# The last 64 channels of the shared expert: high and low rows stacked in one 128-row tile

## The reference

```python
x = x + tanh(g_xattn) * attention(layernorm(x), ctx, ctx, mask)      # 32 heads of 16, 8 groups, causal
x = x + tanh(g_ffn)   * moe(layernorm(x))

# moe, for the 2048 tokens xt (T x 512)
scores  = softmax(xt @ Wg.T)                                         # 16 experts, 4 groups, top 2 groups, top 4
y = sum over the 4 chosen experts e of weight_e * (silu(xt @ W1_e.T) * (xt @ W3_e.T)) @ W2_e.T   # 352 channels
z = (silu(xt @ Ws1.T) * (xt @ Ws3.T)) @ Ws2.T                        # shared expert, 704 channels
moe = y + z
```

## Time and profile before

| | us |
|---|---|
| median of 3 runs | 1259.67 (1258.76 to 1261.95) |
| profiled execution | 1258.79 |
| its span, first to last instruction | 1257.0 |
| PE busy in the span | 1219.0 (97%) |
| PE weight loads busy | 916.7 (73%) |
| VectorE (DVE) busy | 637.5 (51%) |
| ACT busy | 574.3 (46%) |
| POOL busy | 625.3 (50%) |
| `stage_shared` on PE | about 460 to 686 |

### The profile page before, as it was taken

The page is one execution under the profiler, slowest core; times in us unless marked ns, Lnnn a source line. Parts: engine busy times, 40 slices in busy tenths (PEclk is TensorE's granted clock), DMA queues, the critical chain, the costliest instruction groups (busy, mean ns, idle before and its releaser), DMA issues. The chain is left out here.

```text
span 1257.0 us, 23658 instructions
## 1 busy us (share of the span) xinstructions
PE 1219.0 (97%) x7827; PEld 916.7 (73%) x7828; DVE 637.5 (51%) x1831; ACT 574.3 (46%) x986; POOL 625.3 (50%) x662
## 2 busy tenths in 40 slices
PE   8999999999999989999999999999999999999995
PEld 5554555555543467778685899999999999999994
DVE  5347999999956658555240331223333334452100
ACT  2222777777731242222221455545554545555552
POOL 7010333343423324534462576666666666766663
PEclk9999999999989999999999999999999999999998
DMA  9453544444463040010131356565656666665433
GB/s 350 161 175 99 156 132 125 132 127 130 125 177 121 32 171 34 34 42 26 42 128 64 92 138 148 138 148 120 170 117 148 144 167 144 144 144 144 77 65 42
DMA packets 73886, 153.16 MB, mean 122 GB/s; under 512 B 10724, under 2 KB 16356, under 8 KB 73048
## 3 DMA queue, kind: packets, MB, share of 16 engines
q1 hardware_dynamic: 52776, 102.37, 25.1%
q0 software_dynamic: 21040, 49.88, 19.8%
HBM read 97.56 MB, written 52.23 MB: 119 GB/s over the span
## 5 line engine op out<-in xcount | busy, mean ns | idle before, releaser
L1544 DVE CAST e_w<-e_w 128x480 fp32r<-128x480 f32 x135 | 78.2, 580 | 297.8 <-DMA e_w<-in_w2T 293.7
L653 DVE CUSTOM_DVE_ANT_0 a_mb<-a_mb,late 128x512 f32<-128x512 f32 (+1 forms) x480 | 217.4, 529 | 6.4 <-PE a_mb L696 4.6
L1697 PE MATMUL e_yps<-e_w,e_hT 128*128 x711 | 197.2, 404 | 0.9 <-ACT e_hT L1607 0.9
L639 ACT ACTIVATE a_at<-a_eb 128x1024 f32<-128x1024 f32 (+1 forms) x192 | 163.6, 870 | 38.5 <-PE a_eb L717 25.9
L566 POOL TENSOR_SCALAR_AFFINE_SELECT a_at<-a_at 128x256 f32<-128x256 f32 (+1 forms) x192 | 94.6, 493 | 170.4 <-ACT a_at L639 170.4
L1676 PE MATMUL e_up<-e_w,e_xT 128*128 x948 | 170.2, 328 | 0.0
L1676 PE MATMUL e_gate<-e_w,e_xT 128*128 x948 | 167.7, 325 | 1.0 <-issue 1.0
L1676 PEld LDWEIGHTS e_gate<-e_w,e_xT 128*128 128x128 f32 x948 | 155.8, 189 | 11.4 <-issue 6.5
L1676 PEld LDWEIGHTS e_up<-e_w,e_xT 128*128 128x128 f32 x948 | 149.3, 188 | 0.0
L1697 PEld LDWEIGHTS e_yps<-e_w,e_hT 128*128 128x128 f32 x711 | 128.1, 189 | 25.5 <-issue 1.2
L1568 POOL DMA_INDIRECT out<-e_y,scatter x79 | 128.0, 1620 | 23.8 <-issue 14.0
(11 more groups left out here) (263 smaller groups left out, 1838.3 us busy)
## 6 DMA issues: line engine op xcount, KB each, us to landing
e_w<-in_w13T SPq DMA_DIRECT2D x16, 1408.0 KB
dq<-p_parts SPq DMA_DIRECT2D x32, 256.0 KB, 2.4
a_q<-dq SPq DMA_DIRECT2D x64, 128.0 KB
do<-a_o SPq DMA_DIRECT2D x32, 256.0 KB, 2.3
e_w<-in_w2T SPq DMA_DIRECT2D x16, 512.0 KB
a_k<-dk SPq DMA_DIRECT2D x64, 98.0 KB
e_w<-in_ctxT SPq DMA_DIRECT2D x4, 1024.0 KB, 14.4
e_w<-in_x SPq DMA_DIRECT2D x4, 1024.0 KB, 13.2
```

The source lines that it names most:

```text
L639: eng.activation(to, scores, ACT.Exp, scale=0.25).then_inc(s_exp, 1)
L653: eng.tensor_tensor_reduce(out=b[:, 0:w], in0=b[:, 0:w], in1=io["late"][:, SEQ - w:SEQ], scale=1.0, scalar=3 * NEG, op0=ALU.add, op1=ALU.m ...
L1697: mm = eng.matmul(yps[:], hT[r][0:size, mine, n, :], w[0:size, bass.ds(buf, 1), its * SIDE + at:its * SIDE + at + D].rearrange("p b n -> p ...
```

## The change

The last chunk's 64 high rows and 64 low rows of h are stacked in one tile of 128 rows (part 0 of chunk 5), against weights whose high rows stand twice (rows 0 to 63 and 64 to 127) and whose low rows stand once, over 64 rows of zeros. The product of the stack with the doubled high rows is high x high plus low x high; that with the low rows over zeros is high x low. The third pass of chunk 5 is left out, and no matmul of `down` contracts over 64 rows any more. What it adds: a second load of the last 64 rows of Ws2.T by SP, a cast of 128 rows in place of 64 by ACT in `stage_close`, a memset of 64 x 512 on DVE in the second batch of `stage_close`, one copy of 64 x 512 on ACT in each batch of `stage_shared` (from part 1 to rows 64 to 127 of part 0, after the unit of chunk 0), and a semaphore for that copy which PE waits for at the head of the down phase.

```diff
--- before.py
+++ after.py
@@ -801,7 +801,7 @@
         s_den, s_on, s_op, s_x1, s_st, s_mv, s_root, s_newton, s_x2 = (
             sem(f"c_s{n}") for n in ("den", "on", "op", "x1", "st", "mv", "root", "newton", "x2"))
         s_tr, s_xT, s_lg, s_lc, s_whigh, s_wlow = (sem(f"c_s{n}") for n in ("tr", "xT", "lg", "lc", "whigh", "wlow"))
-        s_xhigh, s_part, s_taken = sem("c_sxhigh"), sem("c_spart"), sem("c_staken")
+        s_xhigh, s_part, s_taken, s_pad = sem("c_sxhigh"), sem("c_spart"), sem("c_staken"), sem("c_spad")
         weights = shared_weights(io)
         block = c.enter_context(nc.Block())
 
@@ -817,7 +817,8 @@
             raw = weights[2][2].bitcast(F32)
             eng.dma_start(raw[:, 0:(NS - 1) * D].rearrange("p (c n) -> p c n", c=NS - 1),
                           io["ws2T"][0:(NS - 1) * P].rearrange("(c p) n -> p c n", p=P)).then_inc(s_ws2, 16)
-            eng.dma_start(raw[0:LEFT, (NS - 1) * D:], io["ws2T"][(NS - 1) * P:SHARED]).then_inc(s_ws2, 16)
+            for half in (slice(0, LEFT), slice(LEFT, P)):
+                eng.dma_start(raw[half, (NS - 1) * D:], io["ws2T"][(NS - 1) * P:SHARED]).then_inc(s_ws2, 16)
             eng.wait_ge(s_wlow, KD + 1)
             eng.dma_start(wraw[:, 0:UP].rearrange("p (c n) -> p c n", c=KD), io["wsuT"].rearrange("(c p) n -> p c n", p=P)).then_inc(s_ws[1], 16)
             eng.wait_ge(s_x2, NT + 1)
@@ -835,9 +836,9 @@
                     eng.activation(high, wraw[:, 0:KD * WIDE[n]], ACT.Copy).then_inc(s_whigh, 1)
                 else:
                     at = (NS - 1) * D
-                    eng.wait_ge(s_ws2, 32)
+                    eng.wait_ge(s_ws2, 48)
                     eng.activation(high[:, 0:at], raw[:, 0:at].bitcast(F32), ACT.Copy).then_inc(s_whigh, 1)
-                    eng.activation(high[0:LEFT, at:], raw[0:LEFT, at:].bitcast(F32), ACT.Copy).then_inc(s_whigh, 1)
+                    eng.activation(high[:, at:], raw[:, at:].bitcast(F32), ACT.Copy).then_inc(s_whigh, 1)
 
             eng.wait_ge(s_g, 16)
             eng.activation(tg[:], gx[:], ACT.Tanh).then_inc(s_tg, 1)
@@ -885,8 +886,8 @@
                     eng.tensor_tensor(low[rows, cols], raw[rows, cols], high[rows, cols].bitcast(F32), ALU.subtract).then_inc(s_wlow, 1)
                 if n == 2:
                     eng.wait_ge(s_whigh, 4)
-                    rows, cols = slice(0, LEFT), slice((NS - 1) * D, DOWN)
-                    eng.tensor_tensor(low[rows, cols], raw[rows, cols], high[rows, cols].bitcast(F32), ALU.subtract).then_inc(s_wlow, 1)
+                    cols = slice((NS - 1) * D, DOWN)
+                    eng.tensor_tensor(low[0:LEFT, cols], raw[0:LEFT, cols], high[0:LEFT, cols].bitcast(F32), ALU.subtract).then_inc(s_wlow, 1)
 
             def store(b):
                 eng.wait_ge(s_x2, (b + 1) * CH + 1)
@@ -952,6 +953,9 @@
                 for j in range(CH):
                     eng.bn_aggr(mv[:, j, :], stats[:, j, :]).then_inc(s_mv, 1)
                 inverse_deviation(eng, mv[:, :, 1], root[:], rstd[:], work[:], s_root, s_newton, b)
+                if b == 1:
+                    eng.wait_ge(s_whigh, 4)
+                    eng.memset(weights[2][1][LEFT:, (NS - 1) * D:].bitcast(F32), 0.0).then_inc(s_pad, 1)
                 if b >= 2:
                     eng.wait_ge(s_x2out[b % 2], 16)
                     eng.wait_ge(s_tr, (b - 1) * CH + 1)
@@ -1105,8 +1109,8 @@
         up = [ps(f"s_up{i}", [P, SEQ]) for i in range(2)]
         yps = [ps(f"s_yps{i}", [P, D]) for i in range(2)]
         s_g, s_xT = (dsem(f"s_s{n}") for n in ("g", "xT"))
-        s_tg, s_xhigh, s_xlow, s_gate, s_up, s_act, s_upc, s_raw, s_hhigh, s_hlow, s_down, s_part, s_sum = (
-            sem(f"s_s{n}") for n in ("tg", "xhigh", "xlow", "gate", "up", "act", "upc", "raw", "hhigh", "hlow", "down", "part", "sum"))
+        s_tg, s_xhigh, s_xlow, s_gate, s_up, s_act, s_upc, s_raw, s_hhigh, s_hlow, s_stack, s_down, s_part, s_sum = (
+            sem(f"s_s{n}") for n in ("tg", "xhigh", "xlow", "gate", "up", "act", "upc", "raw", "hhigh", "hlow", "stack", "down", "part", "sum"))
         s_high, s_low = sem("s_shigh"), sem("s_slow")
         block = c.enter_context(nc.Block())
         rows = lambda t, n: t.broadcast_to([P, NT, n])
@@ -1303,7 +1307,7 @@
 
         @block.scalar
         def _(eng):
-            begin(eng, s_exp, s_tg, s_xhigh, s_act, s_upc, s_hhigh, s_part)
+            begin(eng, s_exp, s_tg, s_xhigh, s_act, s_upc, s_hhigh, s_stack, s_part)
             def high_x(b):
                 eng.wait_ge(s_xT, 16 * b)
                 eng.activation(xT[:, 0], xT[:, 1].bitcast(F32), ACT.Copy).then_inc(s_xhigh, 1)
@@ -1332,6 +1336,9 @@
                 if n == order[0] and b:
                     eng.wait_ge(s_down, b * CH + 1)
                 eng.activation(h[0:size, 0, n, :], raw[i % 2][0:size], ACT.Copy).then_inc(s_hhigh, 1)
+                if n == order[1]:
+                    eng.wait_ge(s_hlow, i + 1)
+                    eng.activation(h[LEFT:, 0, NS - 1, :], h[0:LEFT, 1, NS - 1, :].bitcast(F32), ACT.Copy).then_inc(s_stack, 1)
                 if n == order[-1]:
                     for j in range(CH):
                         if b * CH + j < NT - 1:
@@ -1402,10 +1409,11 @@
                 i = b * CH + j
                 for mine, its in PASSES:
                     for n in chunks:
-                        size = SCH[n][1]
+                        if mine and n == NS - 1:
+                            continue
                         first = its * DOWN + n * D
-                        mm = eng.matmul(yps[i % 2][:], h[0:size, mine, n, j * P:(j + 1) * P],
-                                        io["w"][0:size, bass.ds(side[1], 1), first:first + D].rearrange("p b n -> p (b n)"),
+                        mm = eng.matmul(yps[i % 2][:], h[:, mine, n, j * P:(j + 1) * P],
+                                        io["w"][:, bass.ds(side[1], 1), first:first + D].rearrange("p b n -> p (b n)"),
                                         start=not (mine or its) and n == order[0], stop=mine == 1 and n == order[-1], skip_group_check=True)
                 if chunks[-1] == order[-1]:
                     mm.then_inc(s_down, 1)
@@ -1437,6 +1445,7 @@
                 if n == order[-1]:
                     early, late = order[:-1], order[-1:]
                     eng.wait_ge(s_hlow, i + 1)
+                    eng.wait_ge(s_stack, b + 2)
                     for j in range(2):
                         if b or j >= 2:
                             eng.wait_ge(s_part, b * CH + j)
```

## The result

The changed kernel takes 1240.26 us, median of 4 runs (1236.97 to 1241.69), and the kernel before 1259.22 us beside it, median of 4 (1257.25 to 1261.95). The ratio is 0.9834 (95% interval 0.9818 to 0.9849), so the change is worth 19.0 us. That is faster as forecast, and inside the range; the forecast of 1236.7 us was 3.6 us too low. One later execution of the kernel before, 1496.34 us at a mean granted clock of 0.745, was in a slower state and is left out of all ratios and of the medians over several sets.

What follows compares the result with a forecast made beforehand. PE, 97% busy, bounds the kernel, with unseen gaps around 64-row products in the down phase. Per batch 6.20 us less, 0.45 back: 5.75, 23.0 in all; 1258.8 - 23.0 = 1235.8, median 1236.7 us, range 1233.5 to 1241.5.

Steps and rivals of the forecast that it cites:

- Four products a batch, 0.227 us each: PE in stage_shared's down phase: four products fewer a batch at 0.227 us each, 0.91 us a batch.
- 0.43 us a visit, 48 visits, 20.5 us: PE in the down phase: each 64-row product costs 0.43 us beyond itself; twelve visits a batch, 5.12 us.
- 0.45 us a batch for the new wait at j = 2: Down phase: PE waits at token tile j = 2 for ACT's take of j = 0, giving back 0.45 us a batch.
- The slacks: Other waits around the down phase cost nothing: slack 1.9 us for chunk 4, 1.4 for j = 3, 3.1 behind POOL.
- The routing tables: Between stage_shared's units: their first product moves to about 521.1, DVE has written them by 516.1; cost 0, slack 5 us.
- ACT's copy, 0.63 us, hidden: stage_shared: the added copy ahead of chunk 1's silu is covered by ACT's idle time; cost 0, without cover 2.5 us.
- The memset of 64 x 512, taken at 0.5, hidden: stage_close on DVE: bounded by 0.11 and 0.9 us, absorbed by 1.85 us of idle time for PE; cost 0.
- a stretch at 1.2 GHz falls elsewhere: Rival, part given back: slacks used up or a slow stretch, as in stage_close, up to 4.8 us, 1241.5 us; 15%.
- its correction of 0.9 us: Base of the sum: the profiled execution stood 0.9 us under the median of the runs shown, so 1235.8 became 1236.7.

Runs made afterwards that it cites:

- Experiment 2: The changed kernel without the stack: rows 64 to 127 of h's last chunk zeros, 72 products of 128 rows, no ACT copy; 1243.42 us, ratio 0.9871.
- Experiment 3: The kernel before, with the three 64-row products of each token tile in a row ahead of all others; 1247.24 us, ratio 0.9892.
- after: The changed kernel, unaltered, against the kernel before; 1240.26 us at first, ratio 0.9834, then 1241.58, 1240.36 and 1237.93 us.
- experiments 4 and 5: The changed kernel with token tile 1's third pass put behind tile 0's late products, run on two chips; 1238.56 and 1238.06 us.
- experiment 6: The kernel of experiments 4 and 5 plus small products on constants in PE's waits at the head of the experts' stage; 1237.06 us, ratio 0.9812.

## Why the prediction was right, and what it mis-sized

- **Four products a batch, 0.227 us each.** Right: padding against stack, 3.9 us for 3.6.
- **0.43 us a visit, 48 visits, 20.5 us.** Right in kind and size. Experiment 2 took all visits away and gave 18.8 us, which is net of the wait at j = 2: the prediction's own figures make 4 x (5.12 + 0.15 - 0.45) = 19.3. Experiment 3 took 32 away and gave 13.2 (by the prediction 32 x 0.43 = 13.8). The step rested on idle time of the weight loads in the earlier trace rows, while PE itself read as busy for 21.56 of 21.65 us; that reading was the decisive one.
- **0.45 us a batch for the new wait at j = 2.** Right: it stands in the trace as four stretches of 0.52, and covering it gave 0.4 a batch.
- **The slacks.** Right, none was used up. POOL's low part of the next tokens runs from 611.57 to 616.20 us and is done 1.2 us before the first gate load of the next batch, 617.42, as the prediction had it (625.3 against 626.55); no load of L1403 waits for `s_xT`, and j = 3 does not wait. Timeline of ACT there:

```profile
609.00 0.69 ACT L1320 ACTIVATE s_part<-s_yps,s_tg 128x512 f32<-128x512 f32 x1 [4.39 <-PE s_yps L1415]
609.59 1.91 ACT L1313 ACTIVATE s_xT<-s_xT 128x2048 fp32r<-128x2048 f32 x1
611.39 0.68 ACT L1320 ACTIVATE s_part<-s_yps,s_tg 128x512 f32<-128x512 f32 x1
```

- **The routing tables.** Right, though with less to spare than the forecast's 5 us. The first load that reads them starts at 521.87, and DVE had ended them at 517.98 + 1.86 = 519.8, 2.0 us before. Timeline of DVE:

```profile
517.98 1.86 DVE L1256 TENSOR_TENSOR r_atcol<-r_attile,r_put 128x316 f32<-128x316 f32 x2
523.38 1.48 DVE L1248 TENSOR_TENSOR e_x<-r_iotap,r_row 128x512 f32<-128x512 f32 x1 [3.54 <-PE r_tokps L1425]
```

- **ACT's copy, 0.63 us, hidden.** Right. It has its row now, behind the high part of chunk 0:

```profile
519.79 0.63 ACT L1341 ACTIVATE s_h<-s_h 64x512 fp32r<-64x512 f32 x1
```

- **The memset of 64 x 512, taken at 0.5, hidden.** Right: 0.48 us, no 0.11 and no 0.9. What absorbs it is visible too, since DVE's idle time ahead of the next residual fell from 1.85 us to 1.22. Timeline of DVE:

```profile
409.54 0.48 DVE L958 MEMSET e_w<- 64x512 f32 x1 [0.17 <-DVE c_rstd L127]
```

- **The mis-sized step: the clock outside the stage.** The sum held everything behind and ahead of the stage at its old length, and "a stretch at 1.2 GHz falls elsewhere" was a rival with 15% and up to 4.8 us. It happened in every trace of after, at a place the prediction had not named, the seam to the experts, and cost 1.3 us in the means (1.8 in the first pair). The range was met although this term stood at nothing, because the same rival had set the range's upper end. The prediction's argument against it, that the experts' stage is dense, was about the wrong stretch: in the 5.3 us of the seam PEld idles for 1.50 + 0.93 + 0.94 = 3.4. The second part of the miss is the base. By its correction of 0.9 us the forecast stands on the median of three runs, 1259.67, less 23.0; the median of all runs of before is 0.9 us higher. The single trace was further off: its first 40 us had a clock of 0.96 and the start of its stage 1.00, and the three other traces of before were 3.1 to 3.7 us longer. So 3.6 us are 0.3 of the stage, 1.3 of the seam, 0.9 of the base, and 1.1 that no run places.

With four traces of each the account of the spans closes. To the first bridging load, before took 686.5 us in the mean and after 663.9, 22.6 less; behind it after took 1.3 more; the spans are 1259.6 and 1238.4, 21.3 less by the unrounded figures. Over all runs the medians are 1260.6 (35 runs) and 1240.3 (11), 20.3 us apart; the last microsecond between the two is smaller than the scatter of the runs, and its cause is not shown.

**What stays open.** Why the seam falls to 1.2 GHz in after and not in before. The waits at the seam are equal, 5.3 to 5.4 us to the first gate load in both. The kernels of experiments 2 and 3 have the stretch as well in their one trace each (gate loads in 3.43 and 3.00 us; in 2 the 12 up loads behind them take 3.19 us too), those of 4 to 6 do not, and they have no gap in the down phases. No boundary in the span's time parts the two: after has the stretch with its first bridging load at 662.05, 663.53, 663.97 and 666.19 us, and the kernel of 4 and 5 has none with it at 662.92 and 663.23. What PE did in the microseconds ahead of the seam may decide, but before had more gaps there than any, and no stretch. No run tells these apart, and none moves the seam in time while it leaves the work ahead of it and its waits alone, which would test whether the moment matters.

## A version that may beat both

The kernel of experiment 6 has the lowest median measured, 1237.06 us (ratio 0.9812), and that of experiments 4 and 5 is its equal within the scatter, at 1238.06 on the same chip, with a simpler edit. Both are clearly faster than the kernel before; that they are faster than the changed kernel is shown for the stage alone, since the intervals of their ratios overlap with its own (0.9818 to 0.9849). The cover is the part with a shown cause: 1.5 us less in the stage.

## What to carry over

In this kernel a product over 64 rows among products over 128 is dearer than a padded one: pad it with zeros, or better, fill its free rows with another term of the sum. When an engine reads as 97% busy, compare the starts of its weight loads between two stretches of the same kind of product; a difference in pace with idle loads is time that the busy share hides. And take more than one trace of the kernel before as the base of a sum, since its span differed by 3.1 to 3.7 us here between the first trace and the three others, which have stretches at 1.2 GHz that the first had not or had shorter. The median of three runs was nearer, 0.9 us under that of all.

## What the hardware showed that was not expected

- Changing between 64-row and 128-row products costs 0.36 us ahead and 0.24 to 0.37 behind in the idle time of the loads, 0.41 to 0.43 us net for the round trip around one 64-row product. Around three in a row the loads idle by the same 0.36 and 0.37 us, once. Zeros in the other 64 rows cost nothing: both kinds of load take 182 to 192 ns, and padded products follow each other as the full ones do, 36 loads in 8.20 us.
- A stretch at 1.2 GHz can be bound to a place and come every time (four of four traces) in one kernel and never in another whose waits at that place are the same; 28 small products in its waits removed it in the one trace taken, and cost 0.4 us themselves.
